# First group boundary of a fused attention and feed-forward kernel: group 1's keys spread from ScalarE's queue, one mask product and one score product moved

## The reference, cut to what matters

```python
x = x + window_attention(layernorm(x))    # 16 query heads, 2 key/value heads, window of 32
x = x + ffn(layernorm(x))                 # 128 -> 512, butterfly, gelu, butterfly, -> 128
x = x + linear_attention(layernorm(x))
x = x + ffn(layernorm(x))                 # the same weights again
```

```python
kb = concatenate([pk[:, :, :-1], pk[:, :, 1:]], axis=3)      # 64 keys for each block of 32 queries
scores = einsum('bhntd,bhnud->bhntu', qb, kb)
win_mask = (u >= t) & (u < t + W)
probs = softmax(where(win_mask, scores, -inf), axis=-1)
out = einsum('bhntu,bhnud->bhntd', probs, vb)
```

## Time and profile before

| what | value |
|---|---|
| median of 3 runs | 546.55 us (546.4 to 546.69) |
| the profiled execution | 546.01 us |
| its span, first to last instruction | 544.2 us |
| TensorE busy | 95% of the span |
| GpSimd busy | 82% of the span |
| VectorE busy | 78% of the span |
| ScalarE busy | 65% of the span |
| mean granted TensorE clock | 1.0 of full speed |

### The profile page before, as it was taken

The page is one execution under the profiler, slowest core; times in us unless marked ns, Lnnn a source line. Parts: engine busy times, 40 slices in busy tenths (PEclk is TensorE's granted clock), DMA queues, the critical chain, the costliest instruction groups (busy, mean ns, idle before and its releaser), DMA issues.

```text
span 544.2 us, 14354 instructions
## 1 busy us (share of the span) xinstructions
PE 516.2 (95%) x5060; PEld 339.7 (62%) x5060; DVE 425.8 (78%) x1273; ACT 356.3 (65%) x578; POOL 448.7 (82%) x640
## 2 busy tenths in 40 slices
PE   4778888999999999999999999999999999999997
PEld 2454344746657666667667676666676676767765
DVE  5879788998878888787888888888879777844441
ACT  1654447576767677676778777776777777746552
POOL 7538889999989999899899989999989787797241
PEclk9999999999999999999999999999999999999999
DMA  8433323232322313142423223131431312010001
GB/s 304 148 97 91 95 62 87 62 84 51 90 57 51 90 38 84 37 108 47 104 50 91 48 61 83 43 94 45 119 73 42 88 27 64 21 40 20 1 20 40
DMA packets 49559, 38.87 MB, mean 71 GB/s; under 512 B 12368, under 2 KB 38992, under 8 KB 49488
## 3 DMA queue, kind: packets, MB, share of 16 engines
q1 hardware_dynamic: 47040, 33.73, 24.8%
q10 hardware_dynamic: 2448, 4.22, 2.1%
HBM read 15.64 MB, written 5.51 MB: 39 GB/s over the span
## 4 chain that ended last, share of the span: by engine, by line
PE 70%; POOL 15%; issue 4%; DMA 3%; DVE 3%; SPq 2%; ACT 2%; POOLq 0%; DVEq 0%; ACTq 0%
PE ring L807 17%; PE ring L785 16%; PE ps_s L753 8%; PE ring L727 7%; POOL probs_t L614 6%; PE ps_o L770 4%; PE ring L818 4%; PE ring L838 4%; PE ring L888 2%; PE ring L827 2%; PE ring L865 2%; DMA probs_t<-probs_t 1%; POOL xn_P L568 1%; POOL xb_W L584 1%; DMA x_P<-in_x 1%
## 5 line engine op out<-in xcount | busy, mean ns | idle before, releaser
L614 POOL TENSOR_TENSOR probs_t<-probs_t,first 128x1024 f32<-128x1024 f32 x64 | 151.1, 2369 | 19.3 <-DMA probs_t<-probs_t 19.3
L807 PEld LDWEIGHTS ring<-w,early 128*128 128x128 f32 x1024 | 119.1, 192 | 10.0 <-issue 9.0
L1211 ACT ACTIVATE early<-ring,b 128x512 f32<-128x512 f32 x128 | 84.3, 685 | 62.0 <-PE ring L785 61.6
L807 PE MATMUL ring<-w,early 128*128 128x128 f32 x1024 | 119.9, 275 | 1.2 <-ACT early L1211 1.1
L1202 ACT ACT_TABLE_LOAD x58 | 74.4, 1283 | 10.8 <-issue 9.8
L1220 ACT ACTIVATE probs_t<-merged_t 128x1024 f32<-128x1024 f32 x64 | 65.8, 1044 | 11.1 <-DVE merged_t L1579 8.9
L753 PE MATMUL ps_s<-kx,q_t 64*32 64x512 f32 x960 | 64.7, 596 | 2.5 <-DMA kx<-kv_rows 1.6
L1587 DVE STREAM_TRANSPOSE ps_o<-ps_o 128x512 f32<-128x512 f32 x64 | 46.2, 721 | 21.0 <-PE ps_o L770 21.0
L785 PE MATMUL ring<-xT_G,w1b 128*128 128x512 f32 x128 | 60.9, 595 | 0.7 <-ACT xT_G L1192 0.7
L785 PE MATMUL ring<-xT_F,w1b 128*128 128x512 f32 x128 | 60.1, 608 | 0.4 <-ACT xT_F L1192 0.3
L1560 DVE COPY_PREDICATED ps_s<-first,ps_s 128x512 f32<-128x512 uint32 x64 | 44.0, 687 | 17.2 <-PE ps_s L753 16.1
(11 more groups left out here) (126 smaller groups left out, 990.2 us busy)
## 6 DMA issues: line engine op xcount, KB each, us to landing
probs_t<-probs_t SPq DMA_DIRECT2D x256, 64.0 KB, 2.0
kx<-kv_rows SPq DMA_DIRECT2D x120, 40.0 KB, 2.2
x_P<-in_x SPq DMA_DIRECT2D x16, 256.0 KB, 3.1
out_x<-x_G SPq DMA_DIRECT2D x15, 256.0 KB, 2.5
vx_t<-kv_rows SPq DMA_DIRECT2D x128, 8.0 KB
up_s<-in_up_m ACTq DMA_DIRECT2D x7, 256.0 KB, 7.5
down_s<-in_down_m ACTq DMA_DIRECT2D x7, 256.0 KB, 7.5
kv_rows<-kv_t SPq DMA_DIRECT2D x16, 80.0 KB, 2.7
```

Of the source, the lines that this page charges most:

```text
L614: nc.gpsimd.tensor_tensor(parts, parts, keep.rearrange("p (a t) -> p a t", a=1).to_broadcast([P, PAIR * HEADS, WIN]), ALU.mult).then_inc(p ...
L807: last = nc.tensor.matmul(sums[:, P * j:P * (j + 1)], hid[s][:, c, P * j:P * (j + 1)], w2[:, c], start=(c == chunks[0]), stop=(c == chunks ...
L1211: nc.scalar.activation(hid[s][:, c], bank(name)[:], ACT.Gelu, bias=b1[:, c:c + 1]).then_inc(drained[BANK[name]].sem, 1)
```

## The change

Three edits, all in the first turns:

1. `spread_keys(1)`, eight DMAs, leaves SyncE's queue and is issued by ScalarE, between draining X.u3a and `attention_q_out(1)`. Groups 2 to 15 stay on SyncE. On ScalarE, `probs_out(0, 1)` moves ahead of `down_stage_out(1)` and `up_stage_out(4, "a")`.
2. TensorE does S(1,0) ahead of X.d2, X.u5a and X.u5b instead of behind them.
3. GpSimd does um(0,1) ahead of `normalise(2, "P")` instead of behind it. The tables PRODUCTS and PARTED, from which the semaphore values are counted, follow.

```diff
             def spread_keys(g):
                 sp.wait_ge(kv_out.sem, kv_out.after(g, "P.ko"))
-                if g == 1:
-                    sp.wait_ge(kx_cleared, 1)
-                else:
-                    sp.wait_ge(product.sem, product.after(g - 1, *SCORES))
+                sp.wait_ge(product.sem, product.after(g - 1, *SCORES))
...
                 if t == 0:
-                    spread_keys(1)
                     spread_probs(0, 1)
                     spread_probs(0, 2)
                     spread_probs(0, 3)
...
-                for g in due(t, 42, 0, 1):
+                for g in due(t, 42, 1, 1):
                     probs_parted(g, 1)
...
                     up_diagonals()
                     probs_parted(0, 0)
                     ffn_bias()
+                    probs_parted(0, 1)
...
                     up_stage(4, "b")
+                    scores(1, 0)
                     down_stage(2)
                     up_stage(5, "a")
                     up_stage(5, "b")
-                    scores(1, 0)
...
+            def spread_keys(g):
+                act.wait_ge(kv_out.sem, kv_out.after(g, "P.ko"))
+                act.wait_ge(kx_cleared, 1)
+                for h in range(HPK):
+                    act.dma_start(kx[h:P:HPK, h].rearrange("d (j n) -> d j n", j=TILES), keys_of(g)
+                                 ).then_inc(kx_in.sem, 16)
...
                     up_stage_out(3, "b")
                     up_stage_out(3, "a")
+                    spread_keys(1)
                     attention_q_out(1)
+                    probs_out(0, 1)
                     down_stage_out(1)
                     up_stage_out(4, "a")
-                    probs_out(0, 1)
```

## The result

The changed kernel takes 550.92 us, the median of 5 runs (549.49 to 552.47), against 546.55 us (544.57 to 546.69). The ratio is 1.0087 with a 95% interval of 1.0063 to 1.0112: 3.4 to 6.1 us slower, clear of no change (4.8 in the middle; the bare medians differ by 4.4). The forecast was 550.35 us in a range of 548.2 to 552.3. The profiled execution has a span of 549.1 us, 4.9 us more than before.

What follows compares the result with a forecast made beforehand. The start's chain through um(0,1), S(1,3), group 2's keys and S(2,0) sets when TensorE saturates. GpSimd's delay gives +4.3 us, or +3.2 without a long issue; middle 3.8 on 546.55 makes 550.35 us, range 548.2 to 552.3.

Steps and rivals of the forecast that it cites:

- the sum for GpSimd's path: Late tile 1 copies hold um(0,1), then normalise(2) and TensorE's transposes: PV(0,1) 4.3 us late, S(1,3) at 52.7.
- It is covered by the wait that follows: TensorE: S(1,1) slips from 41.38 to about 43.8, hidden by the wait up to 46.9, with 2 us to spare.
- ScalarE becomes the bound: Rival: ScalarE's issues delay the weights chain until S(1,1) is late past 46.9; +5.3 to +6.3 us, chance 0.05.
- This is the edit that costs: GpSimd: um(0,1) ahead of normalise(2) waits for copies landing at 40.8, making PV(0,1) 4.3 us late.
- SyncE's twelve copies: SyncE: E's copies follow ScalarE and end at the same 44.6 as before.
- Nearly free issuing: Rival: ScalarE's key issues cost almost nothing, q_t stays at 32.96; +1.1 to +2.2 us, chance 0.07.
- S(1,0) ahead of three products: TensorE: S(1,0) stands behind X.u4b and starts near 38.1 against 37.98 before; nothing is won.
- Long issues: DMA queues: one issue sometimes takes 1 us more; leaving group 2's keys saves 1.1, falling into ScalarE's eight costs 1.0.
- the odds of 0.4 for any block: Key DMAs: four of the first ten blocks of eight had a long issue; two blocks on the path, none 0.36, one 0.48.
- From there every row is shifted by the same amount: Sign in the changed profile: after S(2,0), near 60.5 to 61.7, all later rows keep one constant shift.
- the shared, locked descriptor generator: ScalarE's key issues beside SyncE's load of group 2's x: 0.5 us more by the rule, left out of the sum.

Runs made afterwards that it cites:

- the pair with and without fillers: The change with GpSimd's order restored, without and with two useless TensorE products ahead of X.u4b: 551.08 and 548.62 us, ratios 1.0102 and 1.0051.
- the first six changed kernels of the table: The change, GpSimd's order undone, TensorE's undone, GpSimd's alone, keys alone, TensorE's alone, against the kernel before: 1.0087, 1.0102, 1.009, 1.0111, 1.0065, 1.0083.

## Why the prediction was right, point by point

The time and the direction were right, and the sum for GpSimd's path was near its rows: the store of the keys landed at 29.90 (29.97 forecast), the eight issues 5.32 us (5.1), q_t 35.30 (35.1), um(0,1) 40.95 (40.85), `normalise(2)` done 47.07 (46.9), S(1,3) 53.17 (52.7).

- **The step that failed** is "It is covered by the wait that follows": S(1,1) was put at 43.8, with 2 us to spare, and came at 46.31. From X.u4b to S(1,1) the forecast had 6.4 us, and it took 8.75. Some 1.6 us of the difference are the fallen clock, which the estimate hadn't (8.80 against 7.20 in the pair with and without fillers). The other 0.8 are the estimate itself, at full clock: X.d3 and X.u6a were put at 1.1 us, and in the profile of before they take 1.5, from 39.55 to 41.06:

```profile
39.55 1.06 PE L922 MATMUL ring<-d_t,down_s 128*128 128x128 f32 x8
40.45 0.61 PE L908 MATMUL ring<-u_t,up_s 128*128 128x129 f32 x4
```

- **What was luck.** The rival "ScalarE becomes the bound" had 0.05 and stood level with the forecast. The time came out only because ScalarE's path, which had been put 2 us shorter, happened to be just as long as GpSimd's: a longer one would have pushed the time up. "This is the edit that costs", said of GpSimd's order, is half the truth: undoing it gives nothing back. E(0,3) came late on the same chain, so SyncE's twelve copies ended at 47.06 and not at 44.6; GpSimd had no idle time behind `normalise(2)`, so that cost nothing here.
- **Nearly free issuing** is out: 0.62 us each on ScalarE, 0.595 on SyncE for the same transfers.
- **S(1,0) ahead of three products** was costed at nothing. By itself it costs 4.5 us.
- **Long issues.** In the profile of the changed kernel the one in group 2's keys is gone (5.08 us for the eight), as was held likelier, and S(2,0) is 3.65 us late. But one of 1.36 us stands at 108.3 in front of a mask product, which idles 0.47 us for it; from there on the shift is 4.2. The rest, up to 4.9, comes behind 160 us: TensorE has one wait of 0.6 us there on VectorE's `merged` that the kernel before doesn't have. What caused that one stays open. Other kernels with the very same program on SyncE took 5.73 and 6.07 us for group 2's keys, so there the long issue is a matter of the execution, and the 1.1 us that the sum gave for it in one case are luck. But the odds of 0.4 for any block, each by itself, don't hold: in all twelve profiles the blocks of groups 8, 10 and 12 have an issue of 0.83 to 1.53 us, those of groups 3, 4 and 5 have none, and group 2's has one in eight of the twelve.
- **The end follows S(1,3).** It was later by 5.0, 5.1, 4.6, 5.2, 2.2 and 3.4 us in the traces of the first six changed kernels of the table, and the times by 4.8, 5.6, 4.9, 6.1, 3.6 and 4.5. The last two traces are the ones whose store landed early; with the 3.7 and 4.6 us estimated above, all six pairs lie within 1 us. "From there every row is shifted by the same amount" held only roughly: behind S(1,3) the shift in these profiles still changed by 1.0 us less to 1.2 us more up to the end, and in the changed kernel it grew from 3.65 us at S(2,0) to 4.9. What adds to it and takes from it there is open, but for the waits named above.

## What to carry to other kernels

An engine's idle time can be filled only by work whose input is there when the idle time begins; work put ahead of something that is ready and wanted delays it for as long as its own input is late. When a join waits for two paths that a change has both lengthened, undoing one of them shows nothing: add each edit alone to the kernel before as well. Before two traces are compared, look whether what arrives ahead of the change arrived at the same time: here a store that landed 2 us sooner made one edit look 1.5 us cheaper than it is. And an idle gap on TensorE can cost twice, once by its length and once by the slow products behind it.

## What the runs showed of the hardware

- After 2.4 us in which TensorE had no product the granted clock was 0.55 in the 2.9 us that followed, and S(1,0) took 1.96 us instead of 1.09. In other runs of this case it fell as well behind waits of 1.75 us (0.58 in the 1.6 us that followed), 1.82 us (0.50 from 37.5 to 40) and 4.10 us (0.53 in 5 us). In the kernel before, whose longest waits from 31 to 60 us are 1.14 us, it stayed at 1.0.
- One of ScalarE's eight issues took 0.80 us and the others 0.62. It started at 30.58, beside SyncE's load of x at 30.57. In five more kernels the one issue beside that load took 0.78 to 0.83, and in the run with the keys alone none did (0.625 at most), where SyncE's own load took 0.63 in place of 0.53. By the rule of the Trainium skill on the shared, locked descriptor generator (Perfetto Trace Analysis, "DMA Instruction — HWDGE (DVE, Sync)") one of two issues waits; the trace agrees, with 0.1 to 0.2 us where up to 0.5 was allowed for. Most issues that overlap don't show it: with half of the keys on each queue, SyncE's four took 0.59 to 0.60 us beside ScalarE's, as long as alone.
- In the twelve profiles the store of group 1's keys, always issued 3.3 us before S(0,3), landed after 1.6 us in two and after 3.0 to 3.7 us in ten. The two are those in which the second of SyncE's copies behind it took 0.59 us and not 1.2 to 1.9.
